# Two steps of the written-out order put later: laying out the score maxima of a cross-attention stage

## The reference

```python
def _attn(q_in, k_in, v_in, wq, bq, wk, bk, wv, bv, wo, bo, causal):
    Q = (q_in @ wq + bq).reshape(Bq, Sq, H, HD)
    ...
    scores = jnp.einsum('bqhd,bkhd->bhqk', Q, Kp) / jnp.sqrt(jnp.float32(HD))
    a = jax.nn.softmax(scores, axis=-1)
    o = jnp.einsum('bhqk,bkhd->bqhd', a, V).reshape(Bq, Sq, Dm)
    return o @ wo + bo
...
x = _layernorm(x + _attn(x, x, x, ..., True), ln1_g, ln1_b)
x = _layernorm(x + _attn(x, encoder_output, encoder_output, ..., False), ln2_g, ln2_b)
x = _layernorm(x + _moe(x, router_w, router_b, e_w1, e_b1, e_w2, e_b2), ln3_g, ln3_b)
```

## Time and profile before

| | us |
|---|---|
| time, median of 3 runs | 758.52 (757.34 to 758.85) |
| the profiled execution: its own time | 757.34 |
| its span, first to last instruction | 755.6 |
| TensorE busy | 712.6 (94%) |
| VectorE busy | 498.8 (66%) |
| ScalarE busy | 369.4 (49%) |
| GpSimd busy | 286.9 (38%) |
| mean granted TensorE clock | 0.981 |

### The profile page before, as it was taken

One profiled execution on the slowest core, in us unless ns is written; L12 is line 12 of the kernel. 1 busy time (PEld: TensorE's weight loads), 2 busy tenths in 40 slices (PEclk: granted clock), 3 DMA queues, 4 the chain that ended last, 5 costly groups with the idle time before them and its releaser, 6 DMA issues.

```text
span 755.6 us, 14560 instructions
## 1 busy us (share of the span) xinstructions
PE 712.6 (94%) x4969; PEld 478.9 (63%) x4969; DVE 498.8 (66%) x1376; ACT 369.4 (49%) x749; POOL 286.9 (38%) x558
## 2 busy tenths in 40 slices
PE   6889999999999999999997899999999999999983
PEld 4444434545464454645563586898999999999941
DVE  5679787678766877656668654465666665666436
ACT  4325465665666676667753446433433333333403
POOL 8305521543653463624653333212332332232114
PEclk9999999999999999999987999999999999999997
DMA  8964421343164021316016873677999999999654
GB/s 273 291 145 129 118 95 46 84 129 128 33 180 127 13 60 49 91 39 183 14 62 216 251 254 98 210 254 239 346 328 342 342 330 338 345 330 336 231 186 164
DMA packets 95154, 140.29 MB, mean 186 GB/s; under 512 B 11855, under 2 KB 81077, under 8 KB 92597
## 3 DMA queue, kind: packets, MB, share of 16 engines
q1 hardware_dynamic: 76357, 107.86, 45.3%
q10 hardware_dynamic: 15072, 22.02, 8.9%
q0 software_dynamic: 3648, 9.45, 3.4%
HBM read 110.65 MB, written 28.65 MB: 184 GB/s over the span
## 4 chain that ended last, share of the span: by engine, by line
PE 76%; DVE 8%; issue 8%; DMA 4%; POOL 2%; ACT 1%; DVEq 0%; SPq 0%; ACTq 0%; POOLq 0%
PE out_acc L984 12%; PE score_pair L961 10%; PE work L932 9%; PE score_pair L855 8%; PE work L849 8%; PE work L906 6%; PE work L855 4%; PE work L1008 4%; DVE neg_part_max L1472 3%; PE score_pair L849 3%; PE work L918 2%; PE work L992 2%; PE work L935 2%; DMA arena<-parts_scratch 1%; PE work L872 1%
## 5 line engine op out<-in xcount | busy, mean ns | idle before, releaser
L1472 DVE TENSOR_REDUCE neg_part_max<-work 128x1 f32<-128x512 f32 (+4 forms) x368 | 213.2, 625 | 66.8 <-PE work L935 36.1
L1244 ACT ACTIVATE arena<-score_pair 128x1024 f32<-128x1024 f32 (+2 forms) x224 | 178.7, 839 | 76.9 <-PE score_pair L961 75.7
L932 PE MATMUL work<-arena 96*128 96x77 bf16 (+4 forms) x640 | 118.2, 277 | 10.7 <-ACT arena L1207 2.7
L984 PE MATMUL out_acc<-arena 128*32 128x512 f32 (+4 forms) x896 | 103.7, 517 | 2.6 <-DVE arena L1492 2.6
L961 PE MATMUL score_pair<-arena 99*128 99x512 bf16 (+2 forms) x448 | 103.9, 337 | 1.0 <-ACT arena L1244 1.0
L1904 POOL DMA_INDIRECT chosen_scratch<-arena,scatter_rows x36 | 35.6, 989 | 174.8 <-DVE arena L1404 174.5
L855 PE MATMUL score_pair<-arena 128*128 128x256 f32 x432 | 97.6, 379 | 0.0
L932 PEld LDWEIGHTS work<-arena 96*128 96x128 bf16 x640 | 49.2, 98 | 74.7 <-issue 30.7
L1960 POOL TENSOR_SCALAR_AFFINE_SELECT arena<-arena 128x256 f32<-128x256 f32 x128 | 51.5, 410 | 118.0 <-ACT arena L1244 116.8
L1177 ACT ACTIVATE arena<-work,expert_b_cols 128x128 f32<-128x128 f32 x180 | 51.1, 369 | 84.2 <-PE work L849 79.4
L849 PE MATMUL work<-arena 128*128 128x128 f32 x720 | 87.2, 278 | 0.1
(11 more groups left out here) (257 smaller groups left out, 958.2 us busy)
## 6 DMA issues: line engine op xcount, KB each, us to landing
arena<-in_L_xattn_e_w SPq DMA_DIRECT2D x54, 1024.0 KB, 6.8
arena<-parts_scratch SPq DMA_DIRECT2D x24, 768.0 KB, 6.0
arena<-in_L_xattn_e_w ACTq DMA_DIRECT2D x18, 1024.0 KB
parts_scratch<-arena_more SPq DMA_DIRECT2D x24, 384.0 KB, 2.6
parts_scratch<-arena_more SPq DMA_DIRECT2D x24, 256.0 KB, 3.0
parts_scratch<-arena_more SPq DMA_DIRECT2D x24, 128.0 KB, 3.0
residual<-in_x SPq DMA_DIRECT2D x4, 512.0 KB, 8.0
tokens_scratch<-residual SPq DMA_DIRECT2D x2, 1024.0 KB, 4.8
```

Of the source, the lines that this page charges most:

```text
L932: m = pe.matmul(bank[:, j * it.w:(j + 1) * it.w], qa[st.half(it.g)][0:R_S, h, n0:n0 + P], k, start=True, stop=not it.last)
L984: m = pe.matmul(o_ps[c * VW:(c + 1) * VW, skip:QG], v, pt[buf][0:rows, j, 0:QG - skip], start=first, stop=last)
L1244: act_e.activation(pt[buf][0:rows, :, 0:w], st2[pair][0:rows, :, 0:w], ACT.Exp, scale=float(HD) ** -0.5).then_inc(pair_taken[pair], 1)
L1472: dve.tensor_reduce(pm[:, it.at, it.t, it.h0:it.h0 + it.nh], bank[:, 0:it.nh * it.w].rearrange("p (j k) -> p j k", j=it.nh), AX.X, ALU.max ...
```

## The change

Both steps belong to stage 7 (cross-attention, batch 1, heads 8 to 15), the last one.

First place (group 0): `lay` stood behind two `out_turn` steps and ahead of two `score` steps of stage 6. It now stands 15 steps later, behind `out_tile`, `out_turn`, `keep`, `weigh`, `normalise`, `v`, `c_prefix`, `c_rank` and the last two `out_tile` of that half, ahead of the fourth `score` of stage 6 group 0. The first `score` of stage 7 group 0, which needs it, stays where it was, 6 steps behind the new place.

Second place (group 1): `gather` stood behind the last `max`, and `lay` seven steps on, behind the second `t_down`. Both now stand side by side behind `r_turn` twice, `weigh`, `normalise`, the second `t_put`, one `r_mul` and one `out_apply`, and ahead of the next `r_mul`. The first `score` that needs them is 8 steps behind the new place.

No instruction is added or dropped. Within the two stretches the work banks of the steps that were passed change by one place.

```diff
-    "R2q2M2Hewq2f2awlqsnqf2Pan2wn2q2n2Kywqfnf2qwfa2SRvhwuMRMRdMRMHt2yq2otoqtzwuvPKo2qSedwuq2Fq2BXwuawax2Oa2xBkxId"
-    "udpdA3rpt2NADWsrNA2lU2so2lt2n3NBn4onUBhVYyUnonNZn3qnqnenha3U2YyR2wuZMaMq2dYR2qwAuq2M2AHNAwudqUwuUd2PZtNtotot"
+    "R2q2M2Hewq2f2awlqsnqf2Pan2wn2q2n2Kywqfnf2qwfa2SRvhwuMRMRdMRMHt2q2otoqtzwuvPKo2yqSedwuq2Fq2BXwuawax2Oa2xBkxId"
+    "udpdA3rpt2NADWsrNA2lU2so2lt2n3NBn4onUBhVYyUnonNZn3qnqnena3U2YR2wuZMahyMq2dYR2qwAuq2M2AHNAwudqUwuUd2PZtNtotot"
```

## The result

| | us |
|---|---|
| before, median | 758.47 (4 runs, 757.34 to 758.85) |
| changed, median | 765.31 (4 runs, 764.0 to 769.72) |
| ratio | 1.0084, 95% interval 1.0054 to 1.0113 |
| forecast | 760.9, range 758.2 to 762.6 |

Slower, as forecast, by some 6.4 us where 2.4 were forecast, and outside the range. A second measurement on another chip, beside 31 runs of the kernel before, gave 1.0076 (1.0043 to 1.0110), that is 5.8 us on 758.9. Single executions of one kernel spread over several us there, so the experiments are read twice: by their ratio (the kernel's median over that of the kernel before, measured beside it), and by distances inside the trace, which repeat to hundredths where nothing was moved.

The account below looks back on a forecast made before the run. TensorE was taken to bound from 482 us on and at the second place, VectorE at 401 to 407 us. First place -0.3, second +1.4, clock +1.3 gave +2.4 us on the median 758.52: 760.9, range 758.2 to 762.6.

Parts of the forecast that it names:

- Which engine bounds where: VectorE bounds at 401 to 407 us, where TensorE has slack; TensorE bounds at 456 to 460 us.
- lateness of TensorE at 461 us is paid one for one: Behind the second place the chain is TensorE's, so nothing gives its lateness back.
- The second place's wait: TensorE waits 2.1 us at lay for gather behind t_put's scatter; 1.4 us later net, 1.8 with the slower gather.
- The score behind it for want of the maxima: Second place: maxima land at 463.8 us, 466.3 by long legs; score comes at about 465.9: hidden, or 0.4.
- b2 late: First place, SyncE's queue: b2 goes out at about 400.7 instead of 395.96 us, costing nothing.
- keep early: First place, SyncE's queue: keep no longer stands behind lay and goes out some us earlier, costing nothing.
- the bank rotation: First place: moves by one place; every bank met was read before TensorE comes to it, so nothing.
- I take 1.3 us, between 0 (it holds) and 2.5: Second place: cost of the clock falling to the low level behind TensorE's new wait, slowing scores, divide and t_down.
- So the stall costs 0 to 2.2, and I take 0: First place: TensorE stalls 1.2 to 3.8 us for the maxima, hidden by VectorE's `first` with 0.3 us to spare.
- so I take 0.3: First place: lay's four transposes leave the front, so out_tile and VectorE's work start earlier, by at most 0.6 us.
- The sum: Both places and the clock: -0.3 + 1.4 + 1.3 = +2.4 us, forecast 760.9.
- both come too late: Rival: group 0's maxima late as well through long DMA legs, normalise late by 1 to 2.2 us; 762.4, chance 0.12.

Follow-up runs that it names:

- e4: Changed kernel plus 34 extra unread bf16 matmuls issued by TensorE just ahead of its wait at lay of group 1; ratio 1.0036 to the kernel before.
- e10: Against the kernel with the second place alone changed: gather of group 1 moved directly ahead of the second t_put; ratio 0.9966 to the kernel before.
- e6: e1 plus 24 extra unread bf16 matmuls issued by TensorE just ahead of its wait for the maxima; ratio 0.9998 to the kernel before.
- changed again: The changed kernel as it is, measured once more beside more runs of the kernel before; ratio 1.0076.
- e1: Changed kernel with the second place put back as before, so only the first lay is late; ratio 1.0019 to the kernel before.
- e3: Changed kernel with gather of group 1 alone put back ahead of the scatter, lay staying late; ratio 0.9993 to the kernel before.

## Why the prediction was off

- Which engine bounds where, and that lateness of TensorE at 461 us is paid one for one: right. From r_turn at 469.95 on it stayed.
- The second place's wait: right in cause, place and size. Forecast 1.4 us net, 1.56 with the clock held (e4), and gone with one move on GpSimd (e10). The wait was 2.34 us for the forecast 2.1.
- The score behind it for want of the maxima, b2 late, keep early, the bank rotation: nothing, as forecast.
- **"I take 1.3 us, between 0 (it holds) and 2.5"**: the term for the clock was too small; this is the step that failed in the second place. The clock fell in all three traces with the unfilled wait and cost 1.7, 1.7 and 3.3 us, the last beyond my bound (which, at 2.5, is 2.6 times the 0.95 of the rows and not "a little more than twice"). I had priced less than the work that TensorE has behind the wait. As for a rule: the Trainium skill (TensorE: Matmul & The Clock Gate, section "Why this matters for your kernels") names a longer idle gap than this one as what brings the low clock back, so by it the clock should have held. The measurement decides: with 2.34 us of waiting among small matmuls the clock fell three times of three.
- **"So the stall costs 0 to 2.2, and I take 0"**: the step that failed in the first place. Two parts of it were off. The read leg took 2.2 us instead of 1.5. It stands in the chain of the changed kernel:

```profile
400.29 2.20 DMA arena<-negmax_scratch
```

  It took 2.1 to 2.3 us in the other five traces with lay late at this place. I had also called this transfer alone, but b2's 1 MB goes out on the same queue 0.48 us behind it (400.77); whether that made it longer is not shown. And I reckoned from the first score to the weigh's end with 4.26 us, the time at the high clock, in the same text that let the clock fall at the other place for the same reason. Filled, the cover is missed by 0.23 us; unfilled, by 1.65. I put the clock on one of two waits only. So the stall costs 1.6 us by D1 where I had 0.
- **"so I take 0.3"**, the gain in front of it: right, 0.44 us where the clock was high. The whole first place is then +1.2 us by the traces and +1.4 by its ratio, where I had -0.3.
- The sum: forecast -0.3 + 1.4 + 1.3 = 2.4. By the ratios 1.4 + 4.3 = 5.7; by the traces 1.2 + 1.6 + 1.7 = 4.5, or 6.1 with the longer low clock. The second measurement's 5.8 lies within that and the first's 6.4 just above; a low clock near the loop in part of the executions, some 2 us each, would fill the gap, which is argued and not shown.
- The rival "both come too late", 762.4 with 0.12, had the right mechanism for the first place, with the long leg alone and not the clock in it; its sum was too small as well, since it carried the same 1.3 for the clock.

Still open: how often the low clock behind lay lasts as long as in the first trace, and so whether the second place costs 3.2 or 4.9 us in the mean; three traces can't tell. Open as well is whether the change makes the low clock near the loop more frequent.

## What to carry to other kernels

When a step is moved in a written-out order, look on every engine for what it is moved past: here four cheap instructions of GpSimd went behind a scatter that waits, and TensorE waited for them. Price a new TensorE wait as two terms, the wait and the clock behind it, and do so at each new wait; a cover of 0.3 us on another engine is none once the work under it may run at half speed. If a wait can't be avoided, independent matmuls issued in it can keep the clock, as in e4, or put its fall off, as in e6.

## What the runs showed of the hardware

- A TensorE wait of 1.4 to 1.7 us in front of the scores was followed by the low clock inside the scores or the weigh behind them in the five traces with it (changed, changed again, e1, e3, e4). 24 matmuls of 128 columns in that wait put it off until scores and weigh were through (e6), where the kernel before has its fall too. At the other place 34 such matmuls avoided it altogether (e4: 1.00 from 460 to 470 us, against 0.62 from 461 to 470 in the changed kernel).
- The way of 24 KB through HBM: the write leg took 1.37 us and the read leg 2.20 us of the changed kernel's chain. The DMA engines were nearly idle in the write leg (share 0.05 at 398 to 400 us); behind the read b2 came on the same queue.
- The scatter by indirect DMA held GpSimd for 1.09 us at this place, and the tensor instruction behind it started at once (458.67 + 1.09 = 459.76, next at 459.77).
